# A transformer block with routed experts on one core: ScalarE scales the next head's probabilities ahead of a cast, and four small router products move behind the attend products of head 10

## The chip, the cores and the metric

The kernel runs on one core of one Trainium2 chip. The core has five engines, each with its own instruction queue that it works through in order: TensorE (PE in the profile, with its weight loads shown apart as PEld), VectorE (DVE), ScalarE (ACT), GpSimd (POOL) and SyncE (SP), which here only starts transfers. They meet through semaphores. The metric is the device time of one execution in microseconds (us); lower is better.

## The reference

Eight sequences of 256 rows of 256 numbers go through a pre-norm transformer block in float32: attention with 16 heads of 128, rotary position code on q and k and a causal mask, then a mixture of 8 experts of which each row takes 2, and a shared expert.

```
def _L0_attn_ref(x, wq, wk, wv, wo):
    q = einsum('bsd,dnh->bsnh', x, wq); k = ... wk; v = ... wv
    q = llama_rope(q);  k = llama_rope(k);  q = q / sqrt(head_dim)
    logits = where(causal, einsum('bqnh,bknh->bnqk', q, k), -1e30)
    probs = softmax(logits)
    return einsum('bqnh,nhd->bqd', einsum('bnqk,bknh->bqnh', probs, v), wo)

def _L0_ffn_ref(hidden_states, gate_w, w1, w3, w2, sw1, sw3, sw2):
    scores = softmax(x @ gate_w.T)
    topk_w, topk_idx = top_k(scores, 2);  topk_w = topk_w / sum(topk_w)
    y_all = einsum('eti,eih->eth', silu(x @ w1[e]) * (x @ w3[e]), w2)
    return sum(y_all[topk_idx, tok] * topk_w) + silu(x @ sw1) * (x @ sw3) @ sw2

x = x + _L0_attn_ref(_layernorm(x), wq, wk, wv, wo)
x = x + _L0_ffn_ref(_layernorm(x), gate_w, w1, w3, w2, sw1, sw3, sw2)
```

## The kernel before

**Numbers as pairs.** TensorE multiplies in the fast float32r form, and exactness is kept by splitting each operand into a high and a low part (`..._hi`, `..._lo`): three products (`three`, L528) stand for one. ScalarE makes each high part with a cast, and VectorE or GpSimd makes the low part by subtracting it from the full value.

**Blocks and heads.** A block is one of the eight sequences, b = 0 (`FIRST`) to 7 (`LAST`). `sequence(b)` is written once for each engine and loops over the 16 heads. It is software-pipelined: in the turn of head h, TensorE transposes the probabilities of head h (L568), makes the scores of head h+2 (L561 and three products of L528), projects q and k of head h+4, makes half a set of values, applies the probabilities of head h to the values ("attend", three products of L528 and L577), and multiplies the result of head h-1 by its output weights. Heads run on over the end of a block, so "h+3" in head 14 is a head of the next block.

**One head's way.** q and k of head h+4 lie in PSUM after the projection. VectorE multiplies them by cosines (L868) and sines (two of L875); GpSimd adds the two (`rope_sum`, L425, in the turn after, as head h+3); ScalarE casts the sum to its high part (`qkt_high`, L1223); GpSimd subtracts for the low part (`low`, L1403); then the scores can be made. VectorE masks them and takes the row maximum (L884), ScalarE takes the exponential and its row sum (`exps`, L1230), VectorE inverts the sum (`invert`, L888), and ScalarE scales the probabilities by it (`normalise`, L1235 and L1236). TensorE transposes them, ScalarE copies the transpose out (L1247, L1248), VectorE makes its low part (`probs_lo`, L896).

**Order on each engine.** It is the order of the code. ScalarE, in the turn of head h: L1247 and L1248 (probabilities of h), the cast of head h+3, normalise of head h+1, exps of head h+2, in odd turns a cast of values (L1219), then the attention result of h (L1263). VectorE: L896 of h, L888 of h+1, L884 of h+2, L868 and L875 of h+4, L901 of h, then what belongs to the block. GpSimd: L425 and L1403 of h+3, then what belongs to the block.

**Work of the block before.** From the second block on, the router of the block before runs between the heads. In head 1 VectorE takes the rows' statistics, in head 2 GpSimd takes the reciprocal root (`rsqrt`, L1397 and L1399) and VectorE then normalises (`rows_norm`, L987). In head 6 VectorE compares the scores of the experts (`compare`, L995), in heads 7 and 8 GpSimd works on the comparisons (L1476, L1481, L1484), after which VectorE sums them to ranks and picks (`rows_rank`, L1001 and L1006). In head 10 TensorE sums the picks over the rows (`ranks`, L672 to L675), for which it waits on `max_done[1]`, the mask and maximum of head 12, because their PSUM bank is shared. In heads 12 to 15 GpSimd writes addresses and starts four indirect transfers (L1516). In head 6 of all but the last block, GpSimd also does a reciprocal root for the next block's rows.

## Time and profile before

| | before |
|---|---|
| median of 3 runs | 813.59 us (812.24 to 814.54) |
| the profiled execution | 814.33 us, its span 812.5 us |
| granted TensorE clock, mean | 0.98 |
| PE busy in the span | 752.0 us, 93% |
| DVE, ACT, POOL busy | 79%, 66%, 59% |
| attention blocks 1 to 6 | 73.4 to 74.3 us each |
| after the last block | from about 631 us on |

The times below are microseconds from the start of the span of that one execution. A row of the timeline has the start, the duration, the engine, the line, the operation, the tiles written and read, and in brackets how long the engine was idle before it and which instruction released it. "x2" is two instructions taken together. Rows for a matmul have a modelled end, and the next one may start before it.

### The profile page before, as it was taken

The numbers are of one execution on the slowest core, as the hardware profiler recorded it, in microseconds if no ns is written. First come the engines' busy times: TensorE is split into PE (matmuls) and PEld (weight loads), VectorE is DVE, ScalarE is ACT, GpSimd is POOL, SyncE is SP. The second block draws the span as 40 slices with busy tenths as digits, with TensorE's granted clock in tenths as the row PEclk, the third lists the DMA queues.
The fourth block names the chain that finished last, engine by engine and source line by source line (L and its number), as shares of the span: only waits on it lengthen the run. The fifth ranks groups of instructions, "written<-read, shape, count | busy, mean of one in ns | idle before, by whom it ended". The sixth has DMA issues, their size and how long they took to land.

```text
span 812.5 us, 16293 instructions
## 1 busy us (share of the span) xinstructions
PE 752.0 (93%) x5520; PEld 701.4 (86%) x5520; DVE 639.6 (79%) x1765; ACT 532.9 (66%) x1663; POOL 482.6 (59%) x508
## 2 busy tenths in 40 slices
PE   3799999999999999999999999999996879999994
PEld 3788999998998999899999989998885868888884
DVE  5698989988897998899888979988995574444447
ACT  4688777767776776777677767677886434555531
POOL 3578666676667666666766676667776261433300
PEclk9899999999999999999999999999999988999997
DMA  7254344444000000000000000001322213333373
GB/s 225 54 170 130 136 184 170 168 163 176 15 1 27 1 14 15 14 14 2 21 8 14 1 28 2 14 14 32 86 73 82 64 40 97 106 106 113 103 246 104
DMA packets 35753, 61.59 MB, mean 76 GB/s; under 512 B 6744, under 2 KB 27192, under 8 KB 35096
## 3 DMA queue, kind: packets, MB, share of 16 engines
q1 hardware_dynamic: 31624, 49.14, 18.6%
q0 software_dynamic: 4048, 11.42, 3.9%
q8 instruction: 45, 0.74, 0.4%
q14 instruction: 36, 0.29, 0.1%
HBM read 47.03 MB, written 32.46 MB: 98 GB/s over the span
## 4 chain that ended last, share of the span: by engine, by line
PE 57%; DVE 19%; POOL 11%; issue 5%; ACT 4%; DMA 3%; SPq 1%; POOLq 0%; DVEq 0%
PE bank L528 44%; DVE work L875 5%; POOL work L425 5%; PE bank L568 3%; POOL qkt_lo L1403 3%; PE bank L561 3%; DVE work L868 2%; PE bank L577 2%; DVE work L884 2%; PE bank L728 2%; POOL rows_by_expert L1516 2%; DVE pt_lo L896 2%; DMA stage<-in_L_attn_wk 1%; ACT qkt_hi L1223 1%; DVE w_lo L842 1%
## 5 line engine op out<-in xcount | busy, mean ns | idle before, releaser
L1403 POOL TENSOR_TENSOR qkt_lo<-work,qkt_hi 128x512 fp32r<-128x512 f32 x128 | 165.7, 1295 | 99.3 <-ACT qkt_hi L1223 99.3
L425 POOL TENSOR_TENSOR work<-work 128x512 f32<-128x512 f32 x127 | 165.3, 1302 | 72.0 <-DVE work L875 64.3
L875 DVE TENSOR_TENSOR work<-bank,sinn 64x512 f32<-64x512 f32 x256 | 176.2, 688 | 3.4
L528 PE MATMUL bank<-xnt_hi,w_lo 128*128 128x256 f32 x512 | 146.9, 287 | 3.2 <-POOL w_lo L1463 3.0
L1223 ACT CAST qkt_hi<-work 128x512 fp32r<-128x512 f32 x128 | 79.5, 621 | 103.1 <-POOL work L425 102.4
L528 PE MATMUL bank<-xnt_hi,w_hi 128*128 128x256 f32 x512 | 146.5, 286 | 0.0
L528 PE MATMUL bank<-xnt_lo,w_hi 128*128 128x256 f32 x512 | 146.5, 286 | 0.0
L1230 ACT ACTIVATE work<-work,bias 128x128 f32<-128x128 f32 (+1 forms) x256 | 112.6, 441 | 0.0
L868 DVE TENSOR_TENSOR work<-bank,cosn 128x512 f32<-128x512 f32 x128 | 87.8, 686 | 22.1 <-PE bank L528 22.0
L528 PEld LDWEIGHTS bank<-xnt_hi,w_lo 128*128 128x128 f32 x512 | 99.6, 195 | 3.9 <-DVE xnt_lo L906 3.3
L528 PEld LDWEIGHTS bank<-xnt_hi,w_hi 128*128 128x128 f32 x512 | 99.9, 195 | 0.0
L528 PEld LDWEIGHTS bank<-xnt_lo,w_hi 128*128 128x128 f32 x512 | 99.9, 195 | 0.0
L528 PE MATMUL bank<-w_hi,att_lo 128*128 128x256 f32 x256 | 82.9, 324 | 0.2 <-DVE att_lo L901 0.2
L528 PE MATMUL bank<-w_hi,xnt_lo 128*128 128x512 f32 (+1 forms) x192 | 73.3, 382 | 8.0 <-DVE xnt_lo L1027 6.9
L1523 POOL DMA_INDIRECT results_by_token<-v_late,stage x39 | 37.6, 963 | 71.9 <-ACT v_late L1319 71.9
L884 DVE CUSTOM_DVE_ANT_0 work<-bank,mask 128x128 f32<-128x128 f32 (+1 forms) x256 | 78.5, 343 | 1.5 <-PE bank L528 1.5
L901 DVE TENSOR_TENSOR att_lo<-bank,att_hi 128x256 fp32r<-128x256 f32 x128 | 54.0, 422 | 30.8 <-ACT att_hi L1263 28.8
L528 PE MATMUL bank<-w_lo,att_hi 128*128 128x256 f32 x256 | 72.3, 282 | 0.0
L528 PE MATMUL bank<-w_hi,xnt_hi 128*128 128x512 f32 (+1 forms) x192 | 72.2, 376 | 0.0
L528 PE MATMUL bank<-w_hi,att_hi 128*128 128x256 f32 x256 | 72.1, 282 | 0.0
L528 PE MATMUL bank<-w_lo,xnt_hi 128*128 128x512 f32 (+1 forms) x192 | 71.4, 372 | 0.0
L568 PE MATMUL bank<-ident,work 128*128 128x128 f32 x384 | 63.8, 274 | 3.6 <-ACT work L1236 3.5
(151 smaller groups left out, 2175.5 us busy)
## 6 DMA issues: line engine op xcount, KB each, us to landing
rows_by_expert<-in_zero_t SPq DMA_DIRECT2D x8, 2056.0 KB
stage<-rows_by_expert SPq DMA_DIRECT2D x39, 128.5 KB
stage<-in_L_ffn_w SPq DMA_DIRECT2D x32, 88.0 KB, 2.0
rows_by_expert<-in_zero_t SPq DMA_DIRECT2D x2, 1028.0 KB
resid<-in_L_attn_x SPq DMA_DIRECT2D x8, 256.0 KB, 3.8
stage<-in_L_attn_wq SPq DMA_DIRECT2D x8, 256.0 KB, 3.4
stage<-in_L_attn_wk SPq DMA_DIRECT2D x8, 256.0 KB, 4.2
stage<-in_L_attn_wv SPq DMA_DIRECT2D x8, 256.0 KB, 3.8
```

The costliest lines, as they stand in the source:

```text
L425: eng.tensor_tensor(roped[:, a], rope_cos[:, a], rope_sin[:, a], ALU.add).then_inc(rope_add, 1)
L528: mm = pe.matmul(out, lhs[a], rhs[b], start=start and n == 0, stop=stop and n == 2, skip_group_check=more)
L561: pe.matmul(p_s[a][:, 0, 0:P], roped[:, a, 0, 0:P], roped[:, a, 1, 0:P], start=True, stop=True)
L568: mm = pe.transpose(p_t[:, k, :], prob[h % 2][:, k * P:(k + 1) * P], ident[:, :])
L868: nc.vector.tensor_tensor(rope_cos[:, a], p_qk[a][:, :, :], c, ALU.mult)
L875: op = nc.vector.tensor_tensor(rope_sin[lo:lo + 64, a], p_qk[a][hi:hi + 64, :, :], sn, ALU.mult)
L884: nc.vector.tensor_tensor_reduce(prob[a][:, cols], p_s[a][:, t, keys], mask[:, m], -SCALE, BIG, ALU.add, ALU.min, bias[:, a, t:t + 1]).the ...
L901: nc.vector.tensor_tensor(att[a][1][:, :], p_o[:, a, :], att[a][0][:, :], ALU.subtract).then_inc(o_lo, 1)
L1223: nc.scalar.copy(qkt[a][0][:, :, :], roped[:, a]).then_inc(qkt_hi, 1)
L1230: nc.scalar.activation(prob[a][:, c], prob[a][:, c], ACT.Exp, bias=bias[:, a, t:t + 1], scale=-1.0, accum_out=rsum[:, a, t:t + 1]).then_in ...
L1403: nc.gpsimd.tensor_tensor(qkt[a][1][:, :, :], roped[:, a], qkt[a][0][:, :, :], ALU.subtract).then_inc(qkt_lo, 1)
L1523: nc.gpsimd.indirect_dma_start(out=res_d, out_offset=bass.IndirectOffsetOnAxis(ap=x_slot[j % ESLOTS][:, D:RW].bitcast(I32), axis=0), in_=y ...
```

## The change

Two pieces of order change, and nothing else: no instruction is added, removed or resized.

```
@@ TensorE, sequence(b), in the turn of head h
-                    if b is not FIRST and h in (4, 5, 10):
+                    if b is not FIRST and h in (4, 5):
                         pe.wait_ge(max_done[1], j0 + h + 3)
                         if h == 4:
                             turn_rows(b, 0)
                         if h == 5:
                             gate_scores(b, 0)
-                        if h == 10:
-                            ranks(b, 0)
                     pe.wait_ge(pt_lo, j0 + h + 1)
...
                     attend(h)
+                    if b is not FIRST and h == 10:
+                        pe.wait_ge(max_done[1], j0 + h + 3)
+                        ranks(b, 0)
@@ ScalarE, sequence(b), in the turn of head h
                     nc.scalar.copy(pts[0][:, :, :], p_t[:, 0:2, :]).then_inc(pt_hi, 1)
+                    if b is not LAST or h + 1 < N:
+                        act.wait_ge(inv_done, j0 + h + 2)
+                        normalise((h + 1) % N)
                     if b is not LAST or h + 3 < N:
                         act.wait_ge(rope_add, j0 + h + 4)
                         qkt_high((h + 3) % N)
-                    if b is not LAST or h + 1 < N:
-                        act.wait_ge(inv_done, j0 + h + 2)
-                        normalise((h + 1) % N)
                     if b is not LAST or h + 2 < N:
                         exps(j0 + h + 2, (h + 2) % N)
```

ScalarE's queue in one turn of a head of a middle block, before; `qkt_hi<-work` is the cast of the rotated rows (the sum of L425), `work<-work,rinv` the two scalings of the probabilities, `work,rsum<-work,bias` the exponentials:

```order
L1248 CAST pt_hi<-bank 128x256
L1223 CAST qkt_hi<-work 128x512
L1235 ACTIVATE work<-work,rinv 128x128
L1236 ACTIVATE work<-work,rinv 128x256
L1230 ACTIVATE work,rsum<-work,bias 128x128
L1230 ACTIVATE work,rsum<-work,bias 128x256
L1263 CAST att_hi<-bank 128x256
```

The same turn of the same engine in the changed kernel, where all lines from here on have a number one higher:

```order
L1249 CAST pt_hi<-bank 128x256
L1236 ACTIVATE work<-work,rinv 128x128
L1237 ACTIVATE work<-work,rinv 128x256
L1224 CAST qkt_hi<-work 128x512
L1231 ACTIVATE work,rsum<-work,bias 128x128
L1231 ACTIVATE work,rsum<-work,bias 128x256
L1264 CAST att_hi<-bank 128x256
```

The cast stood second and stands fourth: between the copy of the probabilities and the exponentials the two scalings have come ahead of it, in every one of the 128 turns but the last.

TensorE's queue in head 10 of a block from the second on, before; `w_hi,xnt_hi` are the values' products, `member,order` the rank products, `pt_hi,v_lo` the first of the attend products, `w_hi,att_lo` the first of the output products:

```order
L528 MATMUL bank<-w_lo,xnt_hi 128x512
L672 MATMUL bank<-member,order 128x16
L673 MATMUL bank<-member,order 128x8
L674 MATMUL bank<-member,order 128x8
L675 MATMUL bank<-member,order 128x8
L528 MATMUL bank<-pt_hi,v_lo 128x256
L528 MATMUL bank<-pt_hi,v_hi 128x256
L528 MATMUL bank<-pt_lo,v_hi 128x256
L577 MATMUL bank<-pt_late,v_late 128x128
L528 MATMUL bank<-w_hi,att_lo 128x256
```

The same place in the changed kernel:

```order
L528 MATMUL bank<-w_lo,xnt_hi 128x512
L528 MATMUL bank<-pt_hi,v_lo 128x256
L528 MATMUL bank<-pt_hi,v_hi 128x256
L528 MATMUL bank<-pt_lo,v_hi 128x256
L577 MATMUL bank<-pt_late,v_late 128x128
L673 MATMUL bank<-member,order 128x16
L674 MATMUL bank<-member,order 128x8
L675 MATMUL bank<-member,order 128x8
L676 MATMUL bank<-member,order 128x8
L528 MATMUL bank<-w_hi,att_lo 128x256
```

The four rank products, with their wait for the maximum of head 12, now stand behind the four attend products and ahead of the output products.

## Rows read from the trace of the kernel before

**Rows 1.** The page: the chain that ended last, by engine.

```profile
PE 57%; DVE 19%; POOL 11%; issue 5%; ACT 4%; DMA 3%; SPq 1%; POOLq 0%; DVEq 0%
```

**Rows 2.** Block 3's window: length; PE, PEld, DVE, ACT, POOL busy; clock, DMA.

```profile
257.80:332.00 74.20, 73.14 (x564) 69.33 (x564) 65.16 (x186) 53.16 (x172) 50.73 (x54) 1.00 0.03 12
```

**Rows 3.** Waits over the whole span: us in total, times, longest us.

```profile
ACT qkt_hi L1223 <- POOL work L425: 102.4, 105, 2.5
...
ACT work L1235 <- DVE rinv L888: 14.0, 40, 0.9
PEld bank L561 <- POOL qkt_lo L1403: 13.1, 18, 5.8
```

**Rows 4.** Timeline of ScalarE, block 3, head 2.

```profile
269.10 0.62 ACT L1223 CAST qkt_hi<-work 128x512 fp32r<-128x512 f32 x1 [0.70 <-POOL work L425]
270.05 0.40 ACT L1235 ACTIVATE work<-work,rinv 128x128 f32<-128x128 f32 x1 [0.33 <-DVE rinv L888]
...
270.75 0.39 ACT L1230 ACTIVATE work<-work,bias 128x128 f32<-128x128 f32 x1
```

**Rows 5.** Timeline of VectorE, block 3, end of head 2 and head 3.

```profile
272.93 1.47 DVE L987 TENSOR_SCALAR xn<-resid,mv,rstd 128x256 f32<-128x256 f32 x2
274.33 0.41 DVE L896 TENSOR_TENSOR pt_lo<-bank,pt_hi 128x256 fp32r<-128x256 f32 x1
274.66 0.15 DVE L888 RECIPROCAL rinv<-rsum 128x2 f32<-128x2 f32 x1
```

**Rows 6.** Timeline of GpSimd, block 3, head 2 and the start of head 3.

```profile
269.80 1.29 POOL L1403 TENSOR_TENSOR qkt_lo<-work,qkt_hi 128x512 fp32r<-128x512 f32 x1 [0.73 <-ACT qkt_hi L1223]
...
271.45 0.72 POOL L1399 TENSOR_TENSOR rstd<-vare,mhalf 128x2 f32<-128x2 f32 x1
272.64 1.29 POOL L425 TENSOR_TENSOR work<-work 128x512 f32<-128x512 f32 x1 [0.47 <-DVE work L875]
```

**Rows 7.** Timeline of TensorE, block 3: scores of head 6, in head 4.

```profile
276.52 0.39 PE L561 MATMUL bank<-work 128*128 128x128 f32 x2
```

**Rows 8.** Instructions that write the tile xn, 285 to 293 us: ns min/median/max.

```profile
L995 DVE TENSOR_TENSOR xn<-pair x2: 210/643/1076, 291.2 to 292.2; 128x64 f32<-128x64 f32 x2
```

**Rows 9.** Timelines of VectorE and GpSimd near the start of the span.

```profile
5.31 0.69 DVE L842 TENSOR_TENSOR w_lo<-stage,w_hi 128x512 fp32r<-128x512 f32 x1 [0.77 <-ACT w_hi L1213]
...
5.00 0.73 POOL L1399 TENSOR_TENSOR rstd<-vare,mhalf 128x2 f32<-128x2 f32 x1
```

**Rows 10.** Timeline of VectorE, block 3, heads 8 and 9.

```profile
296.31 0.16 DVE L888 RECIPROCAL rinv<-rsum 128x2 f32<-128x2 f32 x1
...
300.32 1.01 DVE L1006 TENSOR_TENSOR pick<-rank,route 128x16 f32<-128x16 f32 x2
301.25 0.41 DVE L896 TENSOR_TENSOR pt_lo<-bank,pt_hi 128x256 fp32r<-128x256 f32 x1
```

**Rows 11.** Timelines of ScalarE and GpSimd, block 3, heads 8 and 9.

```profile
296.79 0.62 ACT L1223 CAST qkt_hi<-work 128x512 fp32r<-128x512 f32 x1 [0.85 <-POOL work L425]
...
299.92 1.29 POOL L425 TENSOR_TENSOR work<-work 128x512 f32<-128x512 f32 x1
```

**Rows 12.** Timeline of TensorE, block 3: scores of head 12, ranks, scores of head 13.

```profile
303.86 0.39 PE L561 MATMUL bank<-work 128*128 128x128 f32 x2
...
307.13 0.28 PE L672 MATMUL bank<-member,order 128*128 128x16 f32 x1 [0.39 <-DVE bias L884]
...
309.30 0.39 PE L561 MATMUL bank<-work 128*128 128x128 f32 x2
```

**Rows 13.** Timelines of ScalarE, VectorE, GpSimd and TensorE, block 3, heads 12 to 14.

```profile
315.02 0.62 ACT L1223 CAST qkt_hi<-work 128x512 fp32r<-128x512 f32 x1 [0.20 <-POOL work L425]
...
315.19 0.16 DVE L888 RECIPROCAL rinv<-rsum 128x2 f32<-128x2 f32 x1
...
319.39 1.31 POOL L425 TENSOR_TENSOR work<-work 128x512 f32<-128x512 f32 x1
...
322.77 0.49 PE L561 MATMUL bank<-work 128*128 128x128 f32 x2
```

More of the change, by code:

```diff
@@ L626, in sequence @@
                         transpose_xn(b + 1)
-                    if b is not FIRST and h in (4, 5, 10):
+                    if b is not FIRST and h in (4, 5):
                         pe.wait_ge(max_done[1], j0 + h + 3)
@@ L639, in sequence @@
                     attend(h)
+                    if b is not FIRST and h == 10:
+                        pe.wait_ge(max_done[1], j0 + h + 3)
+                        ranks(b, 0)
                     if h >= 1 or b is not FIRST:
```

8 lines of the change are left out of this document (3 added, 5 removed).

## The prediction

> **What bounds the kernel now.** I read the page's chain first: TensorE holds 57% of it, VectorE 19% and GpSimd 11%, ScalarE 4% [rows 1]. So ScalarE is nowhere late today, and what it may become is the question. The windows come next: in block 3 TensorE is busy 73.14 of 74.20 us, at full clock [rows 2]. A block is close to TensorE's own work, with about 1 us to win and any amount to lose. The waits are third. ScalarE waits 102.4 us for the rotary sum before its cast, 105 times, and then 14.0 us, 40 times, for VectorE's reciprocal before the scaling; TensorE's weight loads wait 13.1 us for the low part that GpSimd makes behind that cast [rows 3]. The reader is to see that the cast stands on a way that TensorE already waits for, and that behind the cast the reciprocal is still late in 40 of 128 turns. Last I read the timeline of block 3, turn by turn; the blocks 1 to 6 repeat it.
>
> **The moved scaling, the rule.** Nothing is added, so the cost lies only in who waits. Now the cast must wait for the reciprocal and the scaling. The reciprocal takes 0.15 us and stands 0.33 behind pt_lo (274.33, 274.66) [rows 5]; a hand-over costs some 0.03; the scalings take 0.70 until the next instruction starts (270.05 to 270.75) [rows 4]. So the cast can start 0.88 after the reciprocal's start. From the cast's start to GpSimd's subtraction are 0.70 (269.10, 269.80), the subtraction takes 1.29 [rows 4, 6], and the scores start 0.05 behind it: a rotary sum that ended at 319.39 + 1.31 = 320.70 was followed by scores at 322.77, and 0.70 and 1.29 leave 0.08 for the two hand-overs [rows 13]. So the scores of a head start no sooner than 2.05 after its cast. Where VectorE is in step with TensorE this hides: in head 8 the reciprocal starts at 296.31, so the cast moves from 296.79 to 297.19, 0.40 later [rows 10, 11]. By the 2.05 the scores of head 11 could then start at 299.2; TensorE starts the next scores in its own order at 303.86 less one head of 4.3, some 299.5 [rows 12], so this is hidden. Where VectorE is behind, because it has the router's work too, it doesn't hide. There are three such places in a block.
>
> **Head 2 to 4.** In head 2 the scaling started at 270.05, released by the reciprocal, after a cast at 269.10 [rows 4]. With the order turned the cast starts at 270.75, 1.65 later. GpSimd's subtraction moves by the same, and with it the reciprocal root behind it, which ended at 271.45 + 0.72 = 272.17 and now ends at 273.82 [rows 6]. VectorE's rows_norm waits for that root. Behind the root GpSimd goes straight on with its rotary sum, which ran at 272.64 for 1.29 and ended at 273.93 [rows 6]; now it runs from 273.8 to 275.1. The two rows_norm took 1.47 together [rows 5], and pt_lo came 0.40 behind the sum's end, at 274.33: the first of them had stood still until GpSimd was through. I take the same here: pt_lo of head 3 at 275.5, reciprocal at 275.83, cast at 276.71, scores of head 6 at 278.76. They started at 276.52 [rows 7]. TensorE loses 2.2 us, and VectorE is in step again after it, since it too waits for those scores.
>
> The standing still is seen best in another place: of the two L995, alike in size, one takes 1.08 us and the other 0.21 [rows 8], and the long one lies over a rotary sum of GpSimd. The Trainium skill (SBUF — State Buffer, "Who interferes with whom") says that VectorE instructions with two SBUF inputs or in a two-port mode share a port pair with GpSimd, and whoever comes second is blocked for the whole instruction. By that rule the sum is the one above; without it rows_norm would end 0.8 us after the root whatever GpSimd does, and the loss would be 1.9 in place of 2.2. This trace agrees with the rule for the sum of L425; but L842, with two SBUF inputs, took an unhindered 0.69 at 5.31 while GpSimd's small L1399 was running from 5.00 to 5.73 [rows 9], so I do not count the root as a blocker.
>
> **Head 6 to 10.** In head 6 the cast comes later too, and the root for the next block behind it pushes the rotary sum of head 10 back beyond L995. L995 should then run freely, some 0.8 us shorter, and head 7 loses nothing. In head 8 the 0.40 passes through GpSimd, which has no gap there, to the rotary sum at 299.92: it ends at 301.61 in place of 301.21 [rows 11]. L1006 took 1.01 for two tiny instructions and pt_lo started 0.04 after the sum's end [rows 10], so pt_lo of head 9 moves to 301.65, its reciprocal to 301.98, the cast to 302.86, and the scores of head 12 to 304.91 against 303.86 [rows 12]: 1.05 later. Here the moved ranks come in. TensorE stood 0.39 idle before them, waiting for the maximum of head 12 [rows 12]. With the scores 1.05 late TensorE reaches this place up to 307.13 - 0.39 - 303.86 = 2.88 after L561, at 307.8 or a little before; the maximum, in VectorE's queue 0.4 later than at 307.1, is there by 307.5. So the wait is gone, and it would be gone in the old order as well. From the ranks to the scores of head 13 are 2.17 of work in either order. New: 304.91 + 2.88 + 2.17 = 309.96 against 309.30 [rows 12], or 309.8 if the modelled end is 0.2 too long. I take a loss of 0.5. The second edit by itself would be worth about 0.4 a block; here it is worth nothing, because the first edit has filled that gap.
>
> **Head 12 to 14.** In head 12 the reciprocal starts at 315.19, so the cast moves from 315.02 to 316.07 [rows 13], 1.05 later. Behind it GpSimd has the addresses and an indirect transfer before its next rotary sum at 319.39, which no wait for VectorE precedes, and the scores at 322.77 follow that sum as closely as a cast and a subtraction allow [rows 13]. GpSimd sets the pace until head 1 of the next block, so the 1.05 is passed on whole. In heads 13 to 0 the scaling runs while ScalarE would have waited for the sum; that makes the exponentials up to 0.7 us earlier, but GpSimd's queue decides there and TensorE gains nothing.
>
> **The sum.** A block from 1 to 6 loses 2.2 + 0.5 + 1.05 = 3.75 us, six of them 22.5. Block 7 has the first two terms but no next block to feed: 2.7. Block 0 has no router work; VectorE and ScalarE split weights there and TensorE has more slack, so I put it at 1 between 0 and 2. What follows the last block has neither edit in it and moves as a whole. Together 26.2: the profiled execution's 814.33 would be 840.5. The median of the runs is 0.74 below that execution, so I predict 839.8 us.
>
> **Bounds.** Below: if rows_norm slips in ahead of GpSimd's sum, head 3's pt_lo stands at 274.7 and the first term is 1.4, not 2.2, 4.8 less over six blocks; if in head 12 half of the delay meets slack that I don't see, 3 less, and block 0 may be 1 less. That is 831, and 828 with the second term at zero in all blocks. Above: if the root does hold the port, L995 waits for the root and then for a whole rotary sum, pt_lo of head 7 comes 0.7 later than it did, and the second term grows by about 1.0: 6 more, 846. A gain is open only if ScalarE's wait for the reciprocal doesn't reach TensorE, which is the first rival.
>
> **The rivals.**
> - Faster. The place is head 10: TensorE no longer stands idle before the ranks, 0.39 us in 7 blocks, 2.7 us, and the scaling done early feeds the transposes sooner. It wins if the low part of the rotated rows has more slack than the cast loses, 1.05 to 1.65 us, in heads 2, 9 and 12. Then the time is about 811. For it speaks that ScalarE is idle for a third of the span and waits 102.4 us for that sum, time into which the scaling would fit [rows 3]. Against it: in the three places the reciprocal comes too late for it, and 2.05 us behind the cast there is no such slack.
> - No change: both edits fall on idle time, 813.6. The same argument speaks against it, and both would have to come out even.
> - A small loss: the delays are real but TensorE makes up most of them, because after one late score VectorE has caught up and the other places then hide. That would leave one of the three terms, 1.05 to 2.2 us in a block: 820 to 828.
> - A larger loss: the port rival of the bounds, 846 and above.
>
> **How the numbers follow.** Measured runs spread by about 0.3%, 2.4 us, and less than that I call the same. Chances: the forecast with its bounds, 828 to 846, 0.80; the small loss 0.08; the larger 0.04; no change 0.02; faster 0.06. That is slower 0.92, same 0.02, faster 0.06. The likeliest case has most of the chance, so the range is its own, 828 to 846, and the small loss and the faster case are what it leaves out.
>
> **What would show it.** In the changed kernel's trace a turn of a middle block shows ScalarE waiting for the reciprocal far more than 40 times and 14.0 us, and for the rotary sum far less than 102.4. TensorE's waits for qkt_lo at L561 grow from 13.1 us by about the whole loss, to 35 or 40 us. Its wait before the rank products is gone. Blocks 1 to 6 last 77.5 to 78.5 us in place of 74.2. rows_norm ends 0.4 behind a rotary sum and L995 has no long one. If blocks are 74 us and the wait at L561 has not grown, I am wrong about the slack behind the cast; if they are 76, one of the three places hides; if they are 79 and L995 is long, the root holds the port.

## The result and the profile after

| | before | after |
|---|---|---|
| median | 813.65 us | 858.91 us (853.54, 853.95, 863.88, 864.89) |
| ratio, 95% interval | | 1.056 [1.047, 1.065] |
| profiled execution, its span | 814.33, 812.5 us | 853.54, 851.7 us |
| block 0 | 80.09 | 87.29 |
| block 1 | 73.46 | 76.75 |
| blocks 2 to 6 | 74.20 to 74.26 | 78.14 to 78.19 |
| block 7, to its head 15 | 75.92 | 86.64 |
| from there to the end | 181.9 | 180.9 |

A block here is the time from TensorE's transposes (L568) of its head 0 to those of the next block's. The kernel is slower, as forecast, but by more than forecast: 858.9 us against 839.8, and above the range's 846. The two profiled executions differ by 39.2 us: 7.2 in block 0, 23.0 in blocks 1 to 6, 10.7 in block 7, and 1.7 less ahead of and behind the blocks. The forecast had 1, 22.5 and 2.7, and nothing for the rest. The changed kernel's four times lie on two levels, 854 and 864, and its profiled execution is of the lower; so 13.0 of the 19.1 us between forecast and median are missing in the profiled execution (853.5 against 840.5), 5.4 come from the median standing between the levels, and 0.7 from the step between profiled execution and median in the kernel before.

The chain of the page after, against [rows 1]: GpSimd's share went from 11% to 24%, VectorE's from 19% to 6%.

```profile
PE 49%; POOL 24%; issue 13%; DVE 6%; ACT 4%; DMA 2%; SPq 0%; POOLq 0%; DVEq 0%
```

The waits of the whole span, against [rows 3] (total, times, longest in us; lines after have a number one higher):

```profile
POOL qkt_lo L1404 <- ACT qkt_hi L1224: 196.9, 128, 4.9
...
ACT work L1236 <- DVE rinv L889: 132.3, 128, 3.3
...
PEld bank L561 <- POOL qkt_lo L1404: 61.5, 63, 5.5
...
ACT qkt_hi L1224 <- POOL work L425: 24.8, 28, 2.1
```

ScalarE now waits for the reciprocal in all 128 turns where it was 40, and for the rotary sum 24.8 us where it was 102.4. The wait moved from the sum to the reciprocal, and the low part behind it is late for TensorE 63 times in place of 18, for 61.5 us in place of 13.1 (forecast 35 to 40).

Windows of block 0, block 3 and block 7 after (length; PE, PEld, DVE, ACT, POOL busy; clock, DMA), against [rows 2]:

```profile
29.30:116.59 87.29, 75.05 (x545) 68.45 (x544) 75.01 (x184) 63.75 (x194) 56.74 (x45) 0.98 0.36 123
271.51:349.70 78.19, 73.86 (x567) 69.52 (x566) 65.39 (x187) 53.57 (x172) 50.31 (x54) 1.00 0.03 11
584.18:670.82 86.64, 68.69 (x484) 60.76 (x483) 67.22 (x172) 57.98 (x189) 56.17 (x62) 0.96 0.24 65
```

and of block 0 and block 7 before:

```profile
30.00:110.09 80.09, 73.97 (x543) 67.84 (x543) 71.41 (x184) 63.78 (x194) 55.74 (x45) 0.98 0.40 135
554.65:630.57 75.92, 65.80 (x482) 60.16 (x483) 61.31 (x171) 59.09 (x189) 55.79 (x62) 0.98 0.27 74
```

Block 3 is 4 us longer for hardly more work (PE 73.86 against 73.14). In block 0 VectorE is busy 3.6 us longer with the same 184 instructions, and in block 7 5.9 us longer with about the same count. The same instructions take longer: they are being held.

**A middle block went as forecast.** Timelines of block 3, heads 2 to 4, after (start, duration, engine, line; in brackets the idle time before and its releaser), of ScalarE, GpSimd, VectorE and TensorE, against [rows 4 to 7]:

```profile
284.38 0.40 ACT L1236 ACTIVATE work<-work,rinv 128x128 f32<-128x128 f32 x1 [1.65 <-DVE rinv L889]
...
285.08 0.60 ACT L1224 CAST qkt_hi<-work 128x512 fp32r<-128x512 f32 x1
```

```profile
287.40 0.72 POOL L1400 TENSOR_TENSOR rstd<-vare,mhalf 128x2 f32<-128x2 f32 x1
288.11 1.28 POOL L425 TENSOR_TENSOR work<-work 128x512 f32<-128x512 f32 x1
```

```profile
288.16 1.71 DVE L988 TENSOR_SCALAR xn<-resid,mv,rstd 128x256 f32<-128x256 f32 x2 [0.81 <-POOL rstd L1400]
289.79 0.41 DVE L897 TENSOR_TENSOR pt_lo<-bank,pt_hi 128x256 fp32r<-128x256 f32 x1
```

```profile
293.02 0.49 PE L561 MATMUL bank<-work 128*128 128x128 f32 x2 [0.88 <-POOL qkt_lo L1404]
```

The cast stands behind the reciprocal, the root behind the cast, the rotary sum behind the root, and pt_lo, the instruction behind rows_norm, starts 0.40 behind the sum's end (289.39). The scores made in the turn of head 4 start at 293.02 against 276.52 in [rows 7], 16.50 us later; those in the turn of head 2 start at 281.99 against 267.66, 14.33 later. So 2.17 us are lost between (forecast 2.2). By the same count the turns 8 to 11 lose 0.57 (forecast 0.5) and the turns 12 to 14 another 1.01 (forecast 1.05).

### The profile page after: what moved, and what is told of

The parts are those of the page before. It is cut to its first block, busy times and chain, and to the rows that moved or that the text cites. A ratio compares the mean times of both kernels' runs of the same rounds, so it can differ in the third digit from the quotient of the medians.

```text
span 851.7 us, 16293 instructions
## 1 busy us (share of the span) xinstructions
PE 760.4 (89%) x5520; PEld 703.8 (83%) x5520; DVE 650.4 (76%) x1765; ACT 533.2 (63%) x1663; POOL 480.9 (56%) x508
## 4 chain that ended last, share of the span: by engine, by line
PE 49%; POOL 24%; issue 13%; DVE 6%; ACT 4%; DMA 2%; SPq 0%; POOLq 0%; DVEq 0%
PE bank L528 38%; POOL qkt_lo L1404 9%; POOL work L425 8%; PE bank L561 3%; POOL w_lo L1464 3%; POOL rows_by_expert L1517 2%; PE bank L568 2%; PE bank L729 2%; PE bank L577 1%; ACT qkt_hi L1224 1%; PE bank L744 1%; DVE work L876 1%; DMA stage<-in_L_attn_wk 1%; DVE work L1080 1%; POOL rstd L1400 1%
## 5 line engine op out<-in xcount | busy, mean ns | idle before, releaser
L425 POOL TENSOR_TENSOR work<-work 128x512 f32<-128x512 f32 x127 | 167.0, 1315 | 16.9 <-DVE work L876 12.4
L1236 ACT ACTIVATE work<-work,rinv 128x128 f32<-128x128 f32 x128 | 51.5, 403 | 132.3 <-DVE rinv L889 132.3
L561 PE MATMUL bank<-work 128*128 128x128 f32 x256 | 57.0, 304 | 46.4 <-POOL qkt_lo L1404 46.4
L1224 ACT CAST qkt_hi<-work 128x512 fp32r<-128x512 f32 x128 | 78.0, 609 | 24.9 <-POOL work L425 24.8
L561 PEld LDWEIGHTS bank<-work 128*128 128x128 f32 x256 | 38.6, 190 | 62.6 <-POOL qkt_lo L1404 61.5
```

Source lines behind the costliest of these rows:

```text
L425: eng.tensor_tensor(roped[:, a], rope_cos[:, a], rope_sin[:, a], ALU.add).then_inc(rope_add, 1)
L561: pe.matmul(p_s[a][:, 0, 0:P], roped[:, a, 0, 0:P], roped[:, a, 1, 0:P], start=True, stop=True)
L1224: nc.scalar.copy(qkt[a][0][:, :, :], roped[:, a]).then_inc(qkt_hi, 1)
L1236: nc.scalar.activation(prob[a][:, 0:P], prob[a][:, 0:P], ACT.Copy, scale=rinv[:, a, 0:1])
```

## The experiments

The blocks of all runs, in us. "Time" is the median of each run's own executions; the blocks are read in its one profiled execution. The kernel before was timed again beside each set of runs, at 812.2 to 813.3, and the ratios below are against that. "h2-10" is the time from head 2 to head 10 of block 0, which leaves out the block's first heads, where a stretch at half clock (granted clock 0.5, 1.2 GHz in place of 2.4) fell in some executions: heads 0 and 1 took 12.2 to 12.4 us where it did (before, after, e1, e2, e5, e11) and 10.1 to 10.8 where it did not (e3, e4, e6, e12, e15, e16). In e1, e4, e10 and e18 another such stretch of 3.4 us falls in head 8, and h2-10 is 47.2 to 47.3 in place of 46.6.

| kernel | time | block 0 | h2-10 | block 1 | block 2 | blocks 3-6 | block 7 |
|---|---|---|---|---|---|---|---|
| before | 813.7 | 80.09 | 40.42 | 73.46 | 74.26 | 74.2 | 75.92 |
| after | 858.9 | 87.29 | 46.56 | 76.75 | 78.18 | 78.2 | 86.64 |
| e1 ScalarE's order alone | 861.2 | 88.51 | 47.26 | 76.75 | 85.02 | 78.2 | 85.76 |
| e2 rank products alone | 809.4 | 80.10 | 40.44 | 72.86 | 73.60 | 73.6 | 76.01 |
| e3 order in blocks 1-6, ranks | 843.6 | 78.11 | 40.43 | 76.75 | 84.11 | 78.2 | 76.61 |
| e4 order in blocks 0, 7 | 829.3 | 86.54 | 47.23 | 73.45 | 74.21 | 74.2 | 85.10 |
| e5 the wait alone, ranks | 832.6 | 85.26 | 44.93 | 74.48 | 75.50 | 75.5 | 81.74 |
| e6 before, VectorE's splits cleared | 809.6 | 74.87 | 37.59 | 73.44 | 74.20 | 74.2 | 73.96 |
| e7 after, the same | 847.4 | 81.54 | 41.30 | 76.76 | 83.57 | 78.1 | 79.28 |
| e8 after, clearing transfers later | 859.6 | 85.95 | 46.56 | 76.76 | 78.16 | 85.6, then 78.2 | 86.23 |
| e9 e2, new order in heads 13 to 0 | 809.1 | 79.52 | 40.45 | 72.23 | 73.64 | 73.6 | 76.55 |
| e10 after, last clearing transfers later | 854.5 | 86.93 | 47.24 | 76.77 | 78.15 | 78.2 | 86.09 |
| e11 before, a copy behind the exps | 814.3 | 81.27 | 41.56 | 73.45 | 74.20 | 74.2 | 76.10 |
| e12 before, the copy in the wait | 814.9 | 78.73 | 40.66 | 73.45 | 74.20 | 74.2 | 76.50 |
| e13 after, GpSimd's splits cut | 852.4 | 81.68 | 42.07 | 76.77 | 78.18 | 78.2 | 81.53 |
| e14 before, the same | 811.2 | 79.04 | 39.61 | 73.41 | 74.23 | 74.2 | 74.11 |
| e15 after, split in the gap | 842.6 | 79.33 | 41.48 | 76.77 | 85.21 | 78.2 | 74.54 |
| e16 e2 in blocks 1-6, e15 in 0, 7 | 808.9 | 79.09 | 41.46 | 72.91 | 73.67 | 73.6 | 73.95 |
| e17 after, old order in head 2 of 1-6 | 852.5 | 85.87 | 46.56 | 75.67 | 82.87 | 77.0 | 86.51 |
| e18 after, old order in head 12 of 1-6 | 853.6 | 86.65 | 47.24 | 75.75 | 82.91 | 77.2 | 85.86 |

A block 2 of 82.9 to 85.2 is the event that the part on the second level of times explains.

**The two edits apart (e1, e2).** In e1 TensorE's edit is undone (the condition below, and `ranks` back at its old place):

```
-                    if b is not FIRST and h in (4, 5):
+                    if b is not FIRST and h in (4, 5, 10):
```

> Only ScalarE's order is changed, the rank products stand where they did. If the rank edit is worth nothing beside the other, as predicted, this is the changed kernel again: some 40 us (or, in its longer runs, 50) over the kernel before, blocks 1 to 6 at 78.2 us, and no wait for the maximum ahead of the ranks. If the rank products cost something behind the attend products, blocks 1 to 6 are shorter than 78.2, and the time below the changed kernel's by 6 times that. If they still gain, blocks are 78.6 or longer.

Measured: ratio 1.060 [1.058, 1.062]. Blocks 3 to 6 are the same as after to 0.02 us: beside ScalarE's edit the rank products are worth nothing, as forecast. In e2 ScalarE's edit is undone and the rank products stay moved:

> Only the rank products move, ScalarE's order is that of before. By the idle 0.39 us ahead of the ranks a block gets 0.3 to 0.6 us shorter: blocks 73.7 in place of 74.2, the kernel 2 to 4 us faster (0.3 to 0.5%). The rival is that VectorE, which is late in head 10, sets the time anyway and the gap opens at the next wait: blocks 74.2 and no change.

Measured: ratio 0.9967 [0.9954, 0.9979], 2.8 us, with 0.6 us for each block from 1 to 6 (forecast by itself: about 0.4). TensorE's timeline of e2, head 10: the rank products follow the attend products with no wait, where they had 0.39 in [rows 12].

```profile
304.75 0.39 PE L577 MATMUL bank<-pt_late,v_late 128*128 128x128 f32 x2
304.89 0.28 PE L673 MATMUL bank<-member,order 128*128 128x16 f32 x1
...
306.48 0.39 PE L561 MATMUL bank<-work 128*128 128x128 f32 x2
```

All of the loss belongs to ScalarE's edit.

**Middle and ends apart (e3, e4).** The new order stands under a condition, `b not in (FIRST, LAST)` in e3, `b in (FIRST, LAST)` in e4 (there without the ranks' move).

> ScalarE's new order in blocks 1 to 6 alone, the old one in block 0 and 7; the rank products are moved. If the costs of the blocks are independent, blocks 2 to 6 are 78.2 us, blocks 0 and 7 are 80 and 76 again, and the kernel is 23 us over the one before (2.8%), which is what I had summed for these blocks (22.5). If block 7's loss is handed on by the blocks ahead of it (or the clock falls because of them), block 7 stays at 80 us or more and the kernel is 28 us or more over.

> ScalarE's new order in blocks 0 and 7 alone; the rank products stand where they did. If the costs are independent, block 0 takes 87 us in place of 80, block 7 86.5 in place of 76, blocks 1 to 6 74.2, and the kernel is 16 to 18 us over the one before (2.1%). I had put these two blocks at 3.7. If the two blocks are only so long because the others are changed too, it is under 8 us. The changed kernel's runs lay at 854 and at 864 us; if the longer ones come from these two blocks (where TensorE waits longest), some of the runs here are 10 us longer than others, and the median up to 27 us over.

Measured: ratios 1.0385 [1.0367, 1.0403] and 1.0213 [1.0195, 1.0231]. The costs of the blocks are independent but for one piece: block 7's heads 0 and 1 take 10.16 us in e3 and 9.52 in e4 (after 10.14, before 9.52), so 0.6 us of block 7's loss come with the order of the block ahead of it. From head 2 to 10, block 0 takes 40.43 us in e3 and 47.23 in e4. The ends alone cost 17 us, as expected. e3 is 31 us over the kernel before and not the 23 expected; 5.9 of that is the event in its block 2.

**The wait without the scalings (e5).**

```
                     if b is not LAST or h + 1 < N:
                         act.wait_ge(inv_done, j0 + h + 2)
-                        normalise((h + 1) % N)
                     if b is not LAST or h + 3 < N:
                         act.wait_ge(rope_add, j0 + h + 4)
                         qkt_high((h + 3) % N)
+                    if b is not LAST or h + 1 < N:
+                        normalise((h + 1) % N)
```

> The cast waits for the reciprocal but stands ahead of the two scalings (ranks moved as in the change). It is then 0.70 us sooner than in the changed kernel; the exponentials are as late as there. By the way of the low part (cast, subtraction, scores) a middle block loses 0.85 in head 3 and 0.35 in head 12 and gains 0.6 by the ranks: 74.8 in place of 78.2. In block 0 and 7, if it is the late scores that cost, most of the 7 and 10 us goes: 82 and 79; if it is the later exponentials, behind which VectorE's attention low part and its weight splits stand, block 0 stays at 85 or more and block 7 at 84 or more. The whole kernel 822 us by the first, 832 or more by the second.

Measured: ratio 1.023 [1.021, 1.026]. The cast starts 0.70 us sooner than after. A middle block keeps 1.25 of its 3.95 us, but block 0 keeps 4.5 of 6.1 in heads 2 to 10, and block 7 keeps 4.1 of 8.5 in heads 2 to 12. The expectation had 74.8 for a middle block (75.5 measured) and 822 us or, by its rival, 832 or more for the whole; it is 832.6, with block 0 as the rival had it (85 or more) and block 7 between the two (79, 84). That the cast waits for the reciprocal at all makes most of block 0's loss and half of block 7's; the 0.70 us of the scalings make the rest.

**Port or queue (e6, e7).** VectorE's weight splits (L843) are longer in block 0 after: their durations add up to 13.66 us in place of 11.39. To see what this holding costs, both kernels get one clearing instruction in place of each split; those low parts are left out.

```
-                    op = nc.vector.tensor_tensor(lo, view(stage[:, n % NSTAGE, :]), hi, ALU.subtract)
+                    op = nc.vector.memset(lo.bitcast(F32), 0.0)
```

> The kernel before with VectorE's weight splits (low part from stage and high part, two SBUF inputs) replaced by writing zeros: it leaves out the low parts of the weights that VectorE makes. It is only there to be compared with the next run. Block 0 gets shorter by up to 5 us, block 7 by up to 3, the rest stays.

> The changed kernel with the same replacement (the same low parts left out). VectorE's splits took 3.3 us longer in block 0 (with the row norms) and 5.7 in block 7 (with rows_norm and compare) than before the change, while GpSimd was busy beside them. If these collisions are what I left out, the difference to the kernel without the change falls in block 0 from 7 to 4 us, in block 7 from 10 to 6. If the loss is the queue order alone (late scores, late exponentials), VectorE's shorter work takes away less than 1.5 us of either difference.

Measured: 809.59 and 847.37 us, ratios 0.995 and 1.042. Block 0 falls by 5.2 in one and 5.75 in the other, so the difference stays at 6.7. In block 7 it falls from 10.7 to 5.3. I read this as "not the port in block 0, but ScalarE's own queue", and that reading was wrong. The 5.2 of e6 hold some 2 us of clock: its heads 0 and 1 had no half-clock stretch (10.17 us, where before had 12.33), while e7's had one (11.77). From head 2 to 10 the difference falls from 6.1 to 3.7 us. So holding VectorE's splits does carry part of the loss, 2.4 us of it, as the expectation's first case had said. In head 4 of e7 pt_lo no longer waits for GpSimd's rotary sum: it starts at 54.39, 0.61 ahead of the sum's end.

**Is it ScalarE's queue (e11, e12)?** The kernel before, with one more copy of 128x512 on ScalarE, in heads 1 to 10 of block 0:

```
+                    if b is FIRST and 1 <= h <= 10:
+                        act.wait_ge(x_in, 16)
+                        nc.scalar.copy(xt2[...], resid[:, 0:ST, :]...)
```

behind the exponentials (e11), or between the cast and the wait for the reciprocal (e12).

> The kernel before, with one more ScalarE copy of 128x512 elements (0.5 to 0.6 us, nothing waits for its result) in heads 1 to 10 of block 0 alone, put behind the exponentials, where ScalarE does not wait. Theory (block 0 is a ring through ScalarE and VectorE, paced by ScalarE's work behind the reciprocal): every head of the ten becomes 0.5 us longer, block 0 grows from 80.1 to 84.5 or 86. Rival (ScalarE is slack in block 0, the loss there came from the later scores): block 0 grows by 1.5 us or less. The whole time grows by as much, the middle blocks stay at 74.2.

> The same extra copy in the same ten heads, but put between the cast and the wait for the reciprocal, where ScalarE stood idle for 0.33 to 0.94 us. Theory of the ring: most of the 0.5 us falls into that wait; block 0 grows by 0.5 to 2 us, at least 2.5 us less than with the copy behind the exponentials. Rival (it is only how much work ScalarE has, whatever its place): both places cost the same.

Measured: ratios 1.001 [1.000, 1.003] and 1.002 [1.000, 1.004]. From head 2 to 10 the copy costs 1.14 us behind and 0.24 ahead. This is read in one trace each; in the times (814.3 and 814.9 us) the two places don't differ. The place matters in these heads as the theory says, but half a microsecond more on ScalarE costs only 0.14 a head, where it should have cost 0.5. So ScalarE's queue doesn't pace block 0 of the kernel before. Whether it does in the changed kernel, these two runs can't say; e13 and e15 do.

**The ring (e13 to e15).** So I followed block 0 turn by turn. VectorE's and GpSimd's timelines of block 0, heads 3 and 4, before:

```profile
50.82 0.41 DVE L896 TENSOR_TENSOR pt_lo<-bank,pt_hi 128x256 fp32r<-128x256 f32 x1
...
54.83 0.94 DVE L842 TENSOR_TENSOR w_lo<-stage,w_hi 128x512 fp32r<-128x512 f32 x1 [0.52 <-ACT w_hi L1213]
55.70 0.41 DVE L896 TENSOR_TENSOR pt_lo<-bank,pt_hi 128x256 fp32r<-128x256 f32 x1
```

```profile
52.00 1.28 POOL L1463 TENSOR_TENSOR w_lo<-stage,w_hi 128x512 fp32r<-128x512 f32 x1
53.93 1.29 POOL L425 TENSOR_TENSOR work<-work 128x512 f32<-128x512 f32 x1 [0.65 <-DVE work L875]
```

and after, of VectorE, ScalarE and GpSimd:

```profile
51.33 0.41 DVE L897 TENSOR_TENSOR pt_lo<-bank,pt_hi 128x256 fp32r<-128x256 f32 x1
51.66 0.15 DVE L889 RECIPROCAL rinv<-rsum 128x2 f32<-128x2 f32 x1
...
55.85 1.68 DVE L843 TENSOR_TENSOR w_lo<-stage,w_hi 128x512 fp32r<-128x512 f32 x1 [0.62 <-ACT w_hi L1214]
57.46 0.41 DVE L897 TENSOR_TENSOR pt_lo<-bank,pt_hi 128x256 fp32r<-128x256 f32 x1
```

```profile
51.84 0.40 ACT L1236 ACTIVATE work<-work,rinv 128x128 f32<-128x128 f32 x1 [2.14 <-DVE rinv L889]
...
52.55 0.60 ACT L1224 CAST qkt_hi<-work 128x512 fp32r<-128x512 f32 x1
```

```profile
53.23 1.27 POOL L1404 TENSOR_TENSOR qkt_lo<-work,qkt_hi 128x512 fp32r<-128x512 f32 x1 [2.38 <-ACT qkt_hi L1224]
54.46 1.28 POOL L1464 TENSOR_TENSOR w_lo<-stage,w_hi 128x512 fp32r<-128x512 f32 x1
55.70 1.29 POOL L425 TENSOR_TENSOR work<-work 128x512 f32<-128x512 f32 x1
```

In both kernels pt_lo starts 0.47 to 0.48 us behind the end of GpSimd's rotary sum (53.93 + 1.29 = 55.22, then 55.70; 55.70 + 1.29 = 56.99, then 57.46), since VectorE's split stands ahead of it and is held while the sum runs. The split takes 0.94 us there before and 1.68 after, and 0.69 where nothing holds it [rows 9]. Before, GpSimd's subtraction and weight split are done by then, and the sum waits 0.65 for VectorE: a turn of 55.70 - 50.82 = 4.88 us. After, the way closes to a ring: pt_lo, reciprocal 0.33, scalings 0.18 later, cast 0.71, subtraction 0.68, weight split 1.23, rotary sum 1.24, its end 1.29, next pt_lo 0.47; that is 6.13 us, which is 57.46 - 51.33. It isn't closed in each turn: in the next one VectorE starts its split ahead of the sum (61.58, the sum at 61.84), the sum is the one held (1.76 us in place of 1.29), and the turn takes 4.90. The eight turns from head 2 to head 10 lose 0.77 on the mean. In e5 the scalings' 0.7 are out of it, and pt_lo goes from 51.31 to 56.78, 5.47. If this is so, taking the weight split out of the ring must give block 0 back. In e13 and e14 GpSimd's splits in the two blocks are cut to a few columns (0.21 to 0.33 us in place of 1.28), the rest left out; VectorE clears the tiles before its first work.

```
+                    x = view(stage[:, n % NSTAGE, :])
+                    if 12 <= n < REST:
+                        x, hi, lo = x[:, ..., 0:8], hi[:, ..., 0:8], lo[:, ..., 0:8]
```

> The changed kernel; GpSimd's weight splits of blocks 0 and 7 take 8 columns of each row in place of all 512 (these low parts are left out, zero in block 0, so the output is not the reference's). Theory: block 0 runs on the ring pt_lo, reciprocal, scalings, cast, GpSimd's subtraction, its weight split, its rotary sum, and only then VectorE's split and the next pt_lo; read in the trace it is 0.33 + 0.18 + 0.71 + 0.68 + 1.24 + 1.24 + 1.29 + 0.46 = 6.13 us for head 3 to 4. Without the 1.24 of the split it is about 5.0: block 0 falls from 87.3 to 80.5 to 83, block 7 from 86.6 to 78 to 82; some 9 to 14 us in all, 840 to 850. Rival (ScalarE's own queue, the cast now behind the reciprocal and before the exponentials, paces block 0, as I read the run with the cleared splits of VectorE): GpSimd's split doesn't matter, block 0 stays at 86 or more.

> The control: the kernel before, with GpSimd's weight splits of blocks 0 and 7 cut to 8 columns in the same way. Theory: the ring is not closed there, since the cast and the subtraction are done before pt_lo; the split runs beside VectorE's products from the score banks: block 0 stays within 1 us of 80.1, block 7 within 2 of 75.9. The difference to the changed kernel in block 0 falls from 7.2 to 3 or less. Rival: both kernels gain alike and the difference stays at 6 or more.

e15 leaves nothing out. GpSimd makes the split behind the rotary sum and behind pt_lo, in the 2.38 us in which it waited for the cast:

```
                         rope_sum(nc.gpsimd, (h + 3) % N)
+                        if b is FIRST or b is LAST:
+                            pool.wait_ge(pt_lo, b * N + h + 1)
+                            split_lo(...)         # GpSimd's split of turn h - 1
                         pool.wait_ge(qkt_hi, j0 + h + 4)
                         low((h + 3) % N)
-                    for n in split_now(b, h - 1): ...
```

> The changed kernel with nothing left out; in blocks 0 and 7 GpSimd makes its weight split of a head not behind the subtraction but before it, behind the rotary sum and behind pt_lo of the same head, in the 2 us in which it waits for the later cast. Theory of the ring: the split's 1.24 us leaves the ring, 6.13 becomes 4.9 to 5.1 a head: block 0 falls from 87.3 to 79.5 to 83, block 7 from 86.6 to 78 to 83, the middle blocks stay at 78.2, together 842 to 848. Rival (ScalarE's queue paces): block 0 at 86 or more. Rival (the moved split delays the subtraction): longer than 87.3.

Measured: 852.4, 811.2 and 842.6 us; ratios 1.048 [1.046, 1.050], 0.998 [0.996, 1.000], 1.036 [1.033, 1.039]. e15's median still has the event in it (its block 2 is 85.21). The profiled execution of e13 took 846.7 us and its other four 851.2 to 852.9, so its median lies above the 840 to 850 expected, and no trace shows what those four had in them. The windows of block 0 and 7 of e15, then its VectorE's and GpSimd's timelines:

```profile
31.40:110.73 79.33, 72.47 (x545) 67.03 (x543) 70.23 (x184) 63.16 (x194) 55.03 (x44) 1.00 0.40 135
585.42:659.97 74.55, 65.30 (x485) 59.36 (x484) 61.40 (x172) 57.22 (x188) 54.22 (x60) 1.00 0.26 72
```

```profile
50.45 0.41 DVE L897 TENSOR_TENSOR pt_lo<-bank,pt_hi 128x256 fp32r<-128x256 f32 x1
...
54.98 0.69 DVE L843 TENSOR_TENSOR w_lo<-stage,w_hi 128x512 fp32r<-128x512 f32 x1 [0.62 <-ACT w_hi L1214]
55.59 0.42 DVE L897 TENSOR_TENSOR pt_lo<-bank,pt_hi 128x256 fp32r<-128x256 f32 x1
```

```profile
50.94 1.29 POOL L1472 TENSOR_TENSOR w_lo<-stage,w_hi 128x512 fp32r<-128x512 f32 x1 [1.56 <-DVE pt_lo L897]
52.36 1.27 POOL L1404 TENSOR_TENSOR qkt_lo<-work,qkt_hi 128x512 fp32r<-128x512 f32 x1
53.58 1.29 POOL L425 TENSOR_TENSOR work<-work 128x512 f32<-128x512 f32 x1
```

The turn is 5.14 us (55.59 - 50.45), VectorE's split is back at 0.69, and VectorE's busy time in block 7 is back at 61.40. With the same work in another place, heads 2 to 10 of block 0 recover 5.1 of the 6.1 us lost, and heads 2 to 12 of block 7 go from 58.39 to 52.87 where before had 49.88: 5.5 of 8.5. The control e14 moved by 0.8 in heads 2 to 10, e13 by 4.5, so the difference between the kernels falls from 6.1 to 2.5. That shows that GpSimd's split in the ring makes most of block 0's loss, and that the ring isn't closed in the kernel before; the last 1.1 us that e15 leaves stay open. Block 0 as a whole looks better than before only because this execution had no half-clock stretch in it (clock 1.00 against 0.98): heads 0 and 1 took 10.32 us against 12.33.

Block 7 falls by 12.1 us in e15, from 86.64 to 74.54, and 6.5 of that are not the ring. They lie in head 14 (10.84 to 4.38 us), where TensorE waits for rows that a transfer brings back from HBM. The first line is of after, the second of e15:

```profile
665.91 0.66 PE L528 MATMUL bank<-w_hi,xnt_lo 128*128 128x352 f32 x1 [5.44 <-DVE xnt_lo L1028]
657.01 0.43 PE L528 MATMUL bank<-w_hi,xnt_lo 128*128 128x352 f32 x1 [0.94 <-DVE xnt_lo L1028]
```

In SyncE's queue that transfer (`cosn<-rows_transposed`, L439) stands behind weight loads that wait for GpSimd's splits. It starts at 662.56 after, 2.58 us behind the transposes of head 14, and at 653.14 in e15, 2.45 ahead of them. The kernel before has the same late transfer (TensorE waits 4.92 us), so this part is a gain of the moved split and not a loss given back. After it the kernel after also ran 6.8 us at half clock (663.8 to 670.6), and e15 did not.

**Where in a middle block (e17, e18).** The old order in head 2 alone, or in head 12 alone, of blocks 1 to 6:

```
+                    old = b is not FIRST and b is not LAST and h == 2      # e18: h == 12
+                    if not old and (b is not LAST or h + 1 < N):
```

> The changed kernel with the old order (cast before the scalings) in head 2 of blocks 1 to 6 alone. The forecast put 2.2 of a middle block's 3.75 us on the cast of this head; the trace after has 2.17 lost between the scores of head 2 and 4. Theory: blocks 1 to 6 fall from 78.17 to 76.0 (75.8 to 76.4). Rival (the loss is a sum over all heads, or moves to head 3 or 4 when head 2 is mended): blocks stay at 77.5 or more.

> The changed kernel with the old order in head 12 of blocks 1 to 6 alone. Forecast for this head: 1.05 us; read after: 1.01. Theory: blocks 1 to 6 fall from 78.17 to 77.1 (77.0 to 77.4). Rival (GpSimd, which sets the pace there, has another way to be late): less than 0.4 us.

Measured: 852.5 and 853.6 us, ratios 1.049 [1.044, 1.054] and 1.051 [1.049, 1.052]. Block 3 of e17, then of e18:

```profile
273.87:350.89 77.02, 73.45 (x567) 69.43 (x565) 65.00 (x187) 53.68 (x172) 50.32 (x54) 1.00 0.03 12
```

```profile
276.43:353.58 77.15, 73.66 (x566) 69.47 (x565) 65.32 (x187) 53.61 (x172) 50.38 (x54) 1.00 0.03 11
```

Head 12 gives 1.0 back, as forecast. Head 2 gives only 1.15, not the 2.2 expected: the scores of the next turn come at 288.68, 4.33 behind those of head 2, but from there to head 4 they take 5.57 where before had 276.52 - 271.99 = 4.53. The remaining 1.0 fits the cast of head 3, which waits for the reciprocal behind rows_norm too, but no run has the old order in both heads. The term of 2.2 would then be two casts, 1.15 and 1.0. The forecast's own working had the second in it (the cast at 276.71); my expectation here forgot it.

**The second level of times (e8, e10).** The profiled execution of the changed kernel is of its lower level, 854 us. All four executions of e1 lie near the upper one, at 860.0 to 861.9, and its trace shows an event that the trace of after has not. GpSimd's, then TensorE's timeline of e1, head 14 of block 1, and windows ahead of it, at it and behind:

```profile
194.76 0.19 POOL L1442 TENSOR_SCALAR xn<-own 128x2 int32<-128x2 f32 x1 [4.76 <-DMA rows_by_expert<-xn,slot]
```

```profile
200.07 0.80 PE L561 MATMUL bank<-work 128*128 128x128 f32 x2 [5.42 <-POOL qkt_lo L1403]
```

```profile
188.90:198.00 9.10, 5.75 (x45) 5.23 (x44) 4.58 (x12) 2.22 (x9) 3.53 (x4) 1.00 0.39 149
199.20:206.00 6.80, 5.93 (x25) 5.64 (x26) 3.43 (x10) 3.85 (x13) 4.57 (x5) 0.50 0.32 135
```

GpSimd waits 4.76 us until the first two indirect transfers have landed, TensorE idles 5.42 waiting for it, and then runs for 6.8 us at the lower of its two levels, 1.2 GHz. Block 2, which has both in it, is 85.0 us instead of 78.2. The traces of e3, e7, e15, e17 and e18 show the same, with 3.4 or 6.8 us at half clock and a block 2 of 5.4 to 7.0 us more. In e8 the transfers that clear the buffer, from the third on, wait for block 1's indirect transfers; in e10 those from the eighth on do (the expectation of e10 says block 3, but the count in the code is reached in block 1):

```
+                if k >= 2:      # e10: k >= 7
+                    sp.wait_ge(scattered, 64)
```

> The changed kernel; only SyncE starts the clearing transfers of 2 MB from the third on after the four scatters of block 1 have landed. In the longer executions (one profile shows it) GpSimd waited 4.8 us in head 14 of block 1 for the first scatters, TensorE stood 5.4 us idle for it and ran at half clock for 6.8 us after. If these scatters queue behind a clearing transfer, the wait is gone in every run, all runs lie at 852 to 855 us, and block 2 is 78.2. If the wait has another cause, runs at 864 still come up.

> The changed kernel, with the clearing transfers from the eighth on held back until block 3's first scatters are through (scattered at 64), the earlier ones as they were. Theory (the higher of the two levels comes from a scatter of block 1 caught behind a clearing transfer that happens to run then; after it GpSimd waits some 4.7 us and TensorE's clock is halved for 6.8 us): no clearing transfer runs by then, block 2 lasts 78.2 us and all runs lie at 852 to 856. Rival (the scatters are late for another reason, the transfers have nothing to do with it): the wait of 4.7 us still appears in some executions, runs up to 862 and more, or its place moves on to blocks 3 or 4 where the last clearing transfers now run.

Measured: ratios 1.056 [1.053, 1.060] and 1.050 [1.047, 1.054]. In e8 the wait left block 1 and came in block 2, where the clearing transfers now ran (block 3 became 85.6); all its four executions, 856.6 to 860.3, lie above the 852 to 855 expected. In e10 it is in no block, and the four executions are 852.2 to 857.7. Two of the changed kernel's own four are as low, so four low ones show little by themselves; the traces of all runs show more.

A clearing transfer beside the indirect ones isn't enough, though: in before and after clearing transfers run through block 1 as well (one starts every 12.6 to 14.1 us), and nothing is late there. What tells the traces apart is the moment. In the seven with the event (e1, e3, e7, e8, e15, e17, e18) GpSimd starts its second indirect transfer 0.7 to 4.0 us after a clearing transfer has started, and its wait ends 10.5 to 13.1 us after that start, when the clearing transfer is nearly over. In the other twelve traces with clearing transfers in block 1 it starts it 10.3 us or more after one, and doesn't wait. So the event depends on the phase between two queues, and any change that shifts block 1 by a few microseconds can bring it or remove it. How the one transfer holds the other is open. That the changed kernel's own upper executions, 863.9 and 864.9, are this event is likely but not shown, since no trace of them exists.

**Better than both (e9, e16).** e9 is e2 with the new order in heads 13 to 15 and 0, where GpSimd sets the pace and the reciprocal is early. e16 is e2 in blocks 1 to 6, and e15 in blocks 0 and 7.

> The rank products stand where the changed kernel has them, and ScalarE scales ahead of the cast only in heads 13, 14, 15 and 0 of a block, where GpSimd and not VectorE sets the pace and ScalarE waits for the rotary sum anyway; everywhere else the cast stays ahead. Theory: in these heads the reciprocal is there before the rotary sum, so the turned order costs no wait; the exponentials come up to 0.7 us earlier, but GpSimd decides there: the time of the rank products alone, 809.4, or 0 to 0.3 us a block less, 807.5 to 809.5. Rival (scaling ahead always costs, since the values' cast and the attended rows stand behind it): 0.3 us or more a block slower than the rank products alone, 811.5 or more.

> The version that the runs point to, nothing left out: the rank products moved; ScalarE's old order (cast, then scalings) in blocks 1 to 6; its new order in blocks 0 and 7, with GpSimd's weight splits moved into the gap before the subtraction. Expected from the parts: block 0 at 79.4 in place of 80.1, blocks 1 to 6 at 73.6 as with the rank products alone, block 7 at 74.6 in place of 76.0; 809.4 less 2.1 is 807.3, 805.5 to 809. Rival (the ends gain nothing in the sum, the tail gives it back): 809 to 811, as with the rank products alone.

Measured: 809.1 and 808.9 us, ratios 0.9951 [0.9934, 0.9968] and 0.9956 [0.9942, 0.9970], against e2's 0.9967. Both beat the kernel before by 0.4 to 0.5%; neither can be told from e2. The forecast for e16 was 807.3. Its block 0 of 79.09 is no gain, since it had no half-clock stretch in heads 0 and 1; from head 2 to 10 it takes 41.46 us where the old order takes 40.42. In block 7 the earlier transfer of head 14 gains 5.3 (9.71 to 4.40) and heads 2 to 12 lose 3.6 against e2 (49.31 to 52.89). What follows is 182.1 us long where e2 has 179.8, but that part varies from 179.8 to 184.7 over all the traces, so whether the gain is given back there is not shown. The rank products' move alone is the version to keep: it is the smallest edit and as fast as the others.

## Why the prediction was wrong, point by point

- *Direction and rule.* Right. "Now the cast must wait for the reciprocal and the scaling": 132.3 us in 128 turns, and where TensorE waits for them the scores start 2.00 to 2.04 us after their cast (forecast 2.05).
- *Head 2 to 4, 2.2.* Measured 2.17. The standing still of rows_norm is there (pt_lo 0.40 behind the sum). e17 shows that head 2's cast makes 1.15 of it.
- *Head 6 to 10, 0.5.* Measured 0.57 in the changed kernel, no wait ahead of the ranks, and both L996 take 0.22 us, so the long one of [rows 8] is gone. That the ranks' move is worth nothing here is shown by e1.
- *Head 12 to 14, 1.05.* Measured 1.01, and 1.0 in e18.
- *Blocks 1 to 6, 3.75 each, 22.5.* Measured 23.0. The way through the three places was right here, not only the number.
- *Block 0, "TensorE has more slack, so I put it at 1 between 0 and 2".* This is the step that failed. It measured 7.2. It was the only term without a turn-by-turn reading, and TensorE's slack isn't what decides there. In its place the runs show a ring: VectorE's weight split is held while GpSimd's rotary sum runs, and the next pt_lo stands behind that split. The rows of before would have shown a turn of 4.88 us that already ran through GpSimd's sum. Putting the cast behind the reciprocal puts three GpSimd instructions, 3.8 us, into that way. With GpSimd's split out of it (e15), heads 2 to 10 recover 5.1 of their 6.1 us.
- *Block 7, 2.7.* Measured 10.7. This step failed in the same way: the term carried the middle blocks' losses over and left the weight splits of this block out. 8.5 us are in heads 2 to 12. e15 takes 5.5 of them away; the 3.0 that stay are near the forecast's 2.7, but no run takes them apart. Of the remaining 2.2, 0.6 lie in heads 0 and 1, which come with block 6's order, and 1.6 at its end, where 6.8 us ran at half clock in place of 3.4.
- *The bounds.* They held for each middle term. The range's upper end took in only the port rival of the middle blocks. The measured median stands 13 us above it: blocks 0 and 7 alone are 14 us over their terms, and the second level of times adds 5.
- *Rivals.* Faster, no change and small loss are out (ratio 1.056). The port rival (the small root holds VectorE) is out too: L996 is short. Its range, 846 and above, holds the measured time, but by luck.

## What to carry to other kernels

Before an instruction is put behind a wait in a queue, follow its results once round to that wait. If they come back to it through other engines, the loss is not the delay but the whole way, in each turn in which it closes; a block with another mix of work has another such way and must be read by itself. Work put into an engine's idle time costs least ahead of the wait: the copy cost 0.24 us in eight heads there (e12) and 1.14 behind it (e11), each read in one trace. And look for a third queue that waits for the moved instruction: moving GpSimd's split also moved a transfer in SyncE's queue, by 5 us against head 14. Last, "more slack there" is no number: the term without rows (block 0) and the term carried over from other blocks (block 7) were the two that missed, by 14 us together.

## What the hardware showed that I had not expected

- A VectorE subtraction with two SBUF inputs took 0.69 us alone, and 1.68 where it started 0.15 behind a GpSimd sum of 1.29 us: it ended 0.54 behind the sum's end. The Trainium skill (SBUF — State Buffer, "Who interferes with whom") says that such a VectorE instruction contends with a GpSimd instruction that reads SBUF, and that the one that comes second is blocked. For GpSimd's large instructions the trace agrees to within 0.15 us, both ways: where the split started first, by 0.26, the sum took 1.76 in place of 1.29. [rows 9] has a small one that held nothing.
- The first two indirect transfers of a block landed late, and GpSimd stood 4.6 to 5.7 us, where the second was started 0.7 to 4.0 us after a transfer of 2 MB within HBM had started (e1, e3, e7, e8, e15, e17, e18); where it was started 10.3 us or more after one (before, after and ten more) they were in time.
- One idle stretch of 5.4 us on TensorE was followed by 6.8 us at the lower clock level (e1). The block with both in it was 6.9 us longer.
